# Vision tower block on one core: sum of squares, reciprocal root and two refining steps placed earlier in the step, and one weight load before the end

## What is computed

```python
h = tok(x) + pos; h = concat([cls_tok, h])                  # 64 x 197 x 256
h = h + attn(layernorm(h))                                  # 16 heads of 16 channels
h = h + ffn(layernorm(h))                                   # 4 experts, 256 -> 1024 -> 256, relu

def stablemax3(l):  l = l - max(l)                          # so l <= 0: the branch `neg`
    s = 1 / (1 - l*(1 - 0.5*l*(1 - l/3)));  return s / sum(s)
def ffn(x):  u = sigmoid(x @ Wu + bu);  k = clip(ceil(4u), 1, 4)
    y_e = relu(x @ W1[e] + b1[e]) @ W2[e] + b2[e]           # e = 0..3
    out = sum over i = 1..4 of where(k >= i, u/i, 0) * y_{(token + i - 1) mod 4}
def layernorm(x):  return (x - mean(x)) / sqrt(var(x) + 1e-5)
```

## Time and profile before

| | us |
|---|---|
| median of 3 runs (4054.66 to 4057.33) | 4057.25 |
| the profiled execution, its own time | 4060.63 |
| its span, first to last instruction | 4058.8 |
| PE busy | 3929.9 (97%) |
| DVE, POOL, ACT busy | 2774.2, 2637.5, 2386.5 |
| PE's granted clock, mean over the span | 0.991 of full |

### The profile page before, as it was taken

The page is one execution under the profiler, slowest core; times in us unless marked ns, Lnnn a source line. Parts: engine busy times, 40 slices in busy tenths (PEclk is TensorE's granted clock), DMA queues, the critical chain, the costliest instruction groups (busy, mean ns, idle before and its releaser), DMA issues.

```text
span 4058.8 us, 84949 instructions
## 1 busy us (share of the span) xinstructions
PE 3929.9 (97%) x29736; PEld 3337.9 (82%) x29736; DVE 2774.2 (68%) x4255; ACT 2386.5 (59%) x4358; POOL 2637.5 (65%) x3419
## 2 busy tenths in 40 slices
PE   7899999999999999999999999999999999999998
PEld 4688888888888888888888888888888888888887
DVE  5666777666767667776667676677766676766753
ACT  5555566655666555666556665556665556655552
POOL 5466666656667666666566666667666666666776
PEclk8899999999999999999999999999999999999999
DMA  5233333333333333333333333333333333333333
GB/s 194 61 98 99 90 105 99 96 105 102 92 102 100 100 99 92 107 99 92 108 102 90 101 100 100 101 95 102 99 97 103 102 93 101 97 101 91 97 107 99
DMA packets 694407, 407.77 MB, mean 100 GB/s; under 512 B 149224, under 2 KB 684648, under 8 KB 692968
## 3 DMA queue, kind: packets, MB, share of 16 engines
q1 hardware_dynamic: 689288, 402.04, 34.8%
q10 hardware_dynamic: 4704, 0.30, 0.1%
HBM read 385.05 MB, written 17.10 MB: 99 GB/s over the span
## 4 chain that ended last, share of the span: by engine, by line
PE 82%; DVE 5%; POOL 5%; ACT 4%; issue 4%; DMA 0%; DVEq 0%; ACTq 0%; POOLq 0%; SPq 0%
PE ps L1213 51%; PE ps L1343 6%; PE ps L1311 5%; PE ps L1296 4%; PE ps L1384 4%; PE ps L1325 4%; PE ps L1393 3%; PE ps L1401 2%; ACT probs L637 2%; ACT probs L646 1%; POOL hT L493 1%; DVE probs L876 1%; DVE rt L920 1%; POOL xn L439 1%; PE ps L1356 1%
## 5 line engine op out<-in xcount | busy, mean ns | idle before, releaser
L1213 PE MATMUL ps<-xn,w1s 128*128 128x197 f32 x4096 | 910.8, 343 | 34.8 <-DVE hT L994 32.9
L1213 PEld LDWEIGHTS ps<-xn,w1s 128*128 128x128 f32 x4096 | 676.9, 189 | 175.1 <-issue 131.9
L1213 PE MATMUL ps<-hT,w_s 128*128 128x197 f32 x4064 | 784.0, 330 | 7.6 <-POOL hT L500 7.4
L876 DVE SCALAR_TENSOR_TENSOR probs<-probs,ps 99x788 f32<-99x788 f32 x512 | 485.6, 970 | 364.2 <-ACT probs L637 364.1
L1213 PEld LDWEIGHTS ps<-hT,w_s 128*128 128x128 f32 x4064 | 692.0, 190 | 9.6 <-issue 8.0
L500 POOL TENSOR_TENSOR hT<-hT 128x197 f32<-128x197 f32 x508 | 319.1, 628 | 572.0 <-ACT hT L617 568.7
L1213 PE MATMUL ps<-xt,w1s 128*128 128x197 f32 x3072 | 685.2, 332 | 3.3 <-ACT hT L608 1.8
L493 POOL TENSOR_SCALAR hT<-hT 128x394 f32<-128x394 f32 x512 | 611.0, 1193 | 14.4 <-DVE hT L994 14.4
L948 DVE TENSOR_REDUCE lows<-ps 99x8 f32<-99x1576 f32 (+1 forms) x256 | 460.8, 1801 | 202.5 <-PE ps L1311 200.4
L1213 PEld LDWEIGHTS ps<-xt,w1s 128*128 128x128 f32 x3072 | 539.6, 190 | 66.1 <-ACT hT L608 3.1
L1213 PE MATMUL ps<-hT,w_a 128*128 128x197 f32 x3048 | 591.0, 329 | 0.2 <-DVE yw L1012 0.2
(11 more groups left out here) (123 smaller groups left out, 5941.7 us busy)
## 6 DMA issues: line engine op xcount, KB each, us to landing
w_a<-in_w SPq DMA_DIRECT2D x384, 256.0 KB, 3.2
w1s<-w_sums SPq DMA_DIRECT2D x512, 192.0 KB, 2.6
w1s<-in_w SPq DMA_DIRECT2D x512, 128.0 KB, 2.3
x<-in_xT SPq DMA_DIRECT2D x30, 1188.0 KB, 5.4
w1s<-in_w SPq DMA_DIRECT2D x512, 64.0 KB, 1.9
w1s<-w_sums SPq DMA_DIRECT2D x512, 64.0 KB, 1.9
out_rows<-rows SPq DMA_DIRECT2D x252, 48.0 KB
hT<-in_w SPq DMA_DIRECT2D x8, 1024.0 KB, 8.5
```

Of the source, the lines that this page charges most:

```text
L876: nc.vector.scalar_tensor_tensor(out=part, in0=part, scalar=3.75, in1=ps[0:HB, 2 * half:2 * half + 2, 0:N], op0=ALU.add, op1=ALU.mult).the ...
L1213: return mm(place, weights, rows, start=start, stop=True, skip_group_check=True)
```

## The change

On POOL, `sum_squares(f)` stands ahead of `relu_2` at s = 2. On ACT, `rs_of(f)` moves from k = 3, behind `up_v(3)`, to the end of k = 2, and at k = 3 `up_v(3)` stands between the two halves of `square`. On DVE, `refine` is cut in two: its first two instructions (L918, L920) go ahead of `poly(3,0)`, and so does `odd_up(3)`; the third (L922) stays ahead of `normal_rows`. At the end, a12 is loaded with a21 into the pixel tile, and `final_products` uses it from there. `load_a` itself is as before. `refine` in the second layer norm, and in the first two steps, keeps its place as `refine_1` followed by `refine_2`. Only orders and one 256 KB load differ; no operation is added to or taken out of the steps.

```diff
 final_a = x[...][:, 0:2 * COUPLES * P].rearrange("p (i g c) -> p i g c", i=2, g=COUPLES)   # was a21
...
                     if n == LAST and s == 8:
                         sp.wait_ge(emb_done, 2 * PAIRS)
-                        sp.dma_start(a21[:], w2[E - 1][:, 0:COUPLES, P:2 * P]).then_inc(a21_in, 16)
+                        sp.dma_start(final_a[:, 0], w2[E - 1][:, COUPLES:2 * COUPLES, 0:P]).then_inc(final_in, 16)
+                        sp.dma_start(final_a[:, 1], w2[E - 1][:, 0:COUPLES, P:2 * P]).then_inc(final_in, 16)
...
@@ POOL, step @@
                         hidden_sums(c - 2)
+                    if s == 2 and has_f and f != 1:
+                        sum_squares(f)
                     if c >= 1 and (has_n or has_t and s < 1):
                         relu_2(c - 1)
                     if s == (1 if f == 1 else 0) and has_f:
                         sum_h(f)
-                    if s == (3 if f == 1 else 2) and has_f:
+                    if s == 3 and f == 1:
                         sum_squares(f)
...
@@ ACT, step, k of the first loop @@
                         square(b, k, 0)
+                    if k in (3,):
+                        relus(1)
+                    if has_b:
                         square(b, k, 1)
...
-                    relus(1)
-                    if k == 3 and has_f:
-                        rs_of(f)
+                    if k not in (3,):
+                        relus(1)
                     if has_b and k > 0:
                         invert(b, k - 1)
...
                     if k == 1 and has_f:
                         squares(f)
+                    if k == 2 and has_f:
+                        rs_of(f)
...
@@ DVE @@
-            def refine(pair, s_rs, s_nt, s_ht, s_rstd):
+            def refine_1(pair, s_rs, s_nt, s_ht):        # L918 and L920
...
+            def refine_2(pair, s_ht, s_rstd):            # L922
...
                 for k in range(8):
                     if k not in (4, 5):
                         even(k)
+                    if k == 3 and has_f:
+                        refine_1(f, rs_ready, nt_ready, ht_ready)
+                    if k == 3:
+                        odd_up(k)
                     if has_b:
                         poly(b, k, 0)
...
-                    if k in (3, 4, 7):
+                    if k in (4, 7):
                         odd_up(k)
...
                     if k == 3 and has_f:
-                        refine(f, rs_ready, nt_ready, ht_ready, rstd_ready)
+                        refine_2(f, ht_ready, rstd_ready)
                         normal_rows(f)
...
@@ PE, final_products @@
-                        if g == 0:
-                            pe.wait_ge(wa_in[(1, 2)[m]], 16 * PAIRS * E)
-                        ins = mm(final_y(m), w_a[:, (1, 2)[m], g], hidden2(c), start=False, stop=g == COUPLES - 1)
+                        if (m, g) == (1, 0):
+                            pe.wait_ge(wa_in[2], 16 * PAIRS * E)
+                        ins = mm(final_y(m), (final_a[:, 0, g], w_a[:, 2, g])[m], hidden2(c), start=False, stop=g == COUPLES - 1)
```

More of the change, by code:

```diff
@@ L227, in vit_block @@
         rows_ready = sem("rows_ready")
-        a21_in = sem("a21_in")
+        final_in = sem("final_in")
         final_done = sem("final_done")
@@ L324, in vit_block @@
         FINAL = PAIRS * E - 1
-        a21 = x[:].rearrange("p a k s -> p (a k s)")[:, 0:COUPLES * P].rearrange("p (g c) -> p g c", g=COUPLES)
+        final_a = x[:].rearrange("p a k s -> p (a k s)")[:, 0:2 * COUPLES * P].rearrange("p (i g c) -> p i g c", i=2, g=COUPLES)
         def final_y(m):
@@ L930, in normal_rows2 @@
             def normal_rows2(b):
-                refine(b, rs2_ready, nt2_ready, ht2_ready, rstd2_ready)
+                refine_1(b, rs2_ready, nt2_ready, ht2_ready)
+                refine_2(b, ht2_ready, rstd2_ready)
                 nc.vector.tensor_tensor(xn2[:, b % 2], hc[:], rstd[:].unsqueeze(1).broadcast_to((P, DK, N)), ALU.mult).then_inc(xn2_ready, 1)
@@ L1048, in first_step @@
                 spread(0, "var", var_done, vt_ready)
-                refine(0, rs_ready, nt_ready, ht_ready, rstd_ready)
+                refine_1(0, rs_ready, nt_ready, ht_ready)
+                refine_2(0, ht_ready, rstd_ready)
                 normal_rows(0)
@@ L1066, in second_step @@
                         q_max_of(0, 1)
-                        refine(1, rs_ready, nt_ready, ht_ready, rstd_ready)
+                        refine_1(1, rs_ready, nt_ready, ht_ready)
+                        refine_2(1, ht_ready, rstd_ready)
                         normal_rows(1)
@@ L1636, in final_products @@
             def final_products():
-                pe.wait_ge(a21_in, 16)
+                pe.wait_ge(final_in, 32)
                 pe.wait_ge(poly_ready, at(PAIRS, 16, 0))
@@ L1642, in final_products @@
                         pe.wait_ge(r1_ready, c + 1)
-                        mm(final_y(m), (w_a[:, 0, g], a21[:, g])[m], hidden(c), start=g == 0, stop=False)
+                        mm(final_y(m), (w_a[:, 0, g], final_a[:, 1, g])[m], hidden(c), start=g == 0, stop=False)
                         pe.wait_ge(r2_ready, c + 1)
-                        if g == 0:
-                            pe.wait_ge(wa_in[(1, 2)[m]], 16 * PAIRS * E)
-                        ins = mm(final_y(m), w_a[:, (1, 2)[m], g], hidden2(c), start=False, stop=g == COUPLES - 1)
+                        if (m, g) == (1, 0):
+                            pe.wait_ge(wa_in[2], 16 * PAIRS * E)
+                        ins = mm(final_y(m), (final_a[:, 0, g], w_a[:, 2, g])[m], hidden2(c), start=False, stop=g == COUPLES - 1)
                     ins.then_inc(final_done, 1)
```

## The result

The changed kernel takes 3984.69 us (median of 4 runs, 3983.49 to 3985.36) against 4056.55 for the one before: ratio 0.9823, 95% interval 0.9806 to 0.984. The profiled execution went from 4060.63 to 3985.05, by 75.6 us where the sum gave 61.7; 3996 was forecast, and 3988 was the lower end of the range. All three waits went as they were meant to; two of them were worth more than I gave them.

The account below looks back on a forecast made before the run. PE, busy 97% of the span, bounds the kernel, so only its waits can be won: 53.9 us in 28 steps, 3.8 in steps 1 and 30, 4.0 at the end, together 61.7, giving 3996 us (8 in 10: 3988 to 4013).

Parts of the forecast that it names:

- Term 1: PE's wait for POOL's sum_squares before the variance goes whole: 0.90 us in the step read, relu_2's delay costing nothing.
- Term 2: PE's wait for DVE's up_sums_2 (even(4)) goes too, 1.06 us a step, once DVE's order is rebuilt.
- my 0.08 of cover: At even(4), PE sees DVE's result at 22.51 and wants it at 22.59, so no wait remains.
- PE would wait 1.96 for an unchanged DVE: At even(4), PE arrives 0.90 us earlier, so without rebuilding DVE's order its wait would be 1.96.
- Term 3: At the end, early a12 removes PE's 2.42 us wait and 1.6 us lost to the half clock: 4.0 together.
- A: DVE's turns with POOL cost more than allowed, leaving some of the second wait: 4009 to 4028 us; chance 0.14.
- B: A third PE wait takes their place, behind gap(4): 4011 us at 0.5 a step; chance 0.10.
- my list of what is late next: Nearest were poly(3) against gap(4), 1.75 us of cover, and odd_up(3) against PE's matmul, 0.7; neither binds.
- C: Slower: refine_1 at DVE's head waits for a late root, delaying odd_up(3), then even(4): 4083 us; chance 0.03.
- D: PE's waits are given back by another engine pacing the step; only the end is won: 4053 us; chance 0.05.
- My lower end: For 8 in 10, 3988 us; the forecast's own 3990 had steps 1 and 2 and their half-clock stretches also gain.

Follow-up runs that it names:

- pool_only: The kernel before with only POOL's swap (sum_squares ahead of relu_2 at s = 2): 4021.32 us, ratio 0.991.
- root_only: The changed kernel without POOL's swap and without the early a12 load, so only root and refining are moved: 4019.5 us, ratio 0.9905.
- end_only: The kernel before with only the early a12 load and its use: 4055.18 us against 4059.52, ratio 0.9991.
- two_swaps_end: The kernel before with POOL's swap, the early a12 load, and even(4) ahead of all of refine on DVE, root unmoved: 4039.81 us, ratio 0.9953.
- root_late: The changed kernel with rs_of back at its old place on ACT, refine_1 still early on DVE: 4060.0 us, ratio 1.0006.

## Why the prediction was right and wrong

**Term 1, the variance: mechanism right, size wrong.** POOL's sum starts at 1973.58, which is 2009.65 in the rows' time (I had 9.68), and the variance waits for nothing. `relu_2`'s delay cost nothing that PE shows. I priced the wait at its idle, 0.90 in that step and 0.87 on average; alone it is worth 1.13 (pool_only and root_only agree). This is the step that failed, and with term 2, where it was made again, it is what put the time below the range: "the wait goes whole" was right, "0.90" as its worth was not.

**Term 2, the second wait: mechanism right, size wrong in two places.** The rebuilt order came out closely. `refine_1` ended at 1980.83, 16.90 in the rows' time (I had 16.92), and took 1.53, not 1.13: the turns with POOL are real. `even(4)` ended at 22.22, 0.23 sooner than I had it. The price was again the idle (1.06 for 1.28). Against that PE came sooner than I reckoned, as term 1 was worth more (the group of matmuls with `even(4)`'s starts at 1985.60, 21.67 in the rows' time, 1.22 earlier and not 0.90), so a rest stayed that shows only in PEld and costs 0.15 a step; my 0.08 of cover did not exist. Net 1.14 a step (2.27 - 1.13).

The statement that PE would wait 1.96 for an unchanged DVE was wrong. ACT's squares of block 3 and all of DVE behind them start from PE's `gap(3)`, and I had the row that shows it: ACT idles 2.07 for that gap.

**Term 3, the end: right in size, its clock part partly luck.** 4.4 us in the profiles, 4.0 forecast (2.4 of wait and 1.6 of clock). The wait was worth 2.7, again its idle (2.42) and some more. The half clock was worth 1.7, but I took it from one execution: those of pool_only and root_only have the same wait and kept the full clock. So the wait alone does not bring it about; what decides is not shown. In the medians this part need not be whole.

**The sum.** 28 steps: 63.5 for 53.9, 9.6 short. The end: 4.4 for 4.0. The remaining steps and the start: 7.8 for 3.8. Of this last, two steps at 2.27 are 4.5, and the rest, some 3 us, is not accounted for. It lies where the clock falls to half in places, ahead of the 28 steps and behind them. (The full clock of before ends at 3932, not at 3943 as I wrote: over 3932 to 3937 it was 0.66.) In end_only, which changes nothing ahead of the last pair, the fourth mean matmul started at 265.45 instead of 271.27, so that stretch moves by up to 6 us from one execution to another; neither this rest nor the profile's gain over the median's (75.6 against 71.9) is laid to the change.

**Rivals.** A did not come about, though the turns did. Nor did B in the changed kernel: no wait on a new line. In two_swaps_end it did, before the q projection, a place that my list of what is late next did not have. C was made real by root_late and has the place and the order of waits that I gave it; there it ate the gain and no more. D fell. My lower end came from "half-clock stretches also gain" and not from a doubt about the price of a wait, which I had not bounded from above.

The Trainium skill's rule (SBUF — State Buffer, Who interferes with whom), that a DVE instruction with two SBUF inputs and a GpSimd one that reads SBUF contend, holds in these rows: L925, L927 and L937 took 0.71, 0.78 and 1.54 beside POOL. It holds for POOL's one-input `relu_2` too, which took 1.50 behind L927 and 1.19 in the step's other place. The refining of the second layer norm in the trace before, with POOL idle, shows the same instructions alone: 0.56, 0.57, 0.57 and, for the rows, 0.98:

```profile
2100.12 0.56 DVE L918 TENSOR_TENSOR rt<-rt,rstd 128x394 f32<-128x394 f32 x1
...
2100.72 0.57 DVE L920 SCALAR_TENSOR_TENSOR rt<-rt,rstd 128x394 f32<-128x394 f32 x1
2101.32 0.57 DVE L922 SCALAR_TENSOR_TENSOR rstd<-rt,rstd 128x394 f32<-128x394 f32 x1
2101.92 0.98 DVE L932 TENSOR_TENSOR xn<-hc,rstd 128x788 f32<-128x788 f32 x1
```

## What to carry to other kernels

Where PE bounds, a wait costs more than the idle that the profile shows. Here, with matmuls of 197 and 394 columns, it was a quarter of a microsecond more each, and the weight load's wait was an upper bound in every kernel of the table (2.53 for 2.41). What a change was worth is read from the length of a step between two equal marks, not from busy shares or from counts over a stretch that is no whole number of steps. A half-clock stretch seen in one execution is to be looked for in a second one before it is priced. Before a chain is moved, look which instruction at the head of the list blocks which: one exchange of two DVE instructions gave nearly all that moving the root gave, and with the same instruction still further up, ahead of the refining, most of the gain was lost, since the instruction put first was not ready. An engine that hangs on PE's own output moves with PE when PE gets faster.

## What the runs showed of the hardware that I had not expected

A wait of TensorE cost 0.20 to 0.26 us beyond its shown idle, at lengths from 0.38 to 1.56. In the variance's place the rows show 0.17 of overlap between neighbouring matmuls (whose ends are modelled), and 0.11 behind the restart. And a weight load that waited 0.28 a step while PE showed no idle still cost 0.15. Why a restarted matmul is slower was not tried.
